# Spreading softmax reciprocals as a high and a low part by two one-pass products instead of one four-byte product

## The reference

```python
def _gqa(q, k, v):
    scale = 1.0 / np.sqrt(q.shape[-1])
    scores = jnp.einsum('bsghd,btgd->bghst', q, k) * scale
    p = jax.nn.softmax(scores, axis=-1)
    return jnp.einsum('bghst,btgd->bsghd', p, v)
...
xout = _gqa(qx, kx, vx).reshape(b, s, nh * d)
cat = jnp.concatenate([core, xout], axis=-1)
catq = _div_clamp_fp8(cat, proj_smooth)
```

## Time and profile before

| what | value |
|---|---|
| median of 3 runs | 2472.32 us (2472.16 to 2473.99) |
| the profiled execution, own time | 2472.09 us |
| its span, first to last instruction | 2470.4 us |
| PE busy | 2306.3 us, 93% |
| DVE busy | 1999.1 us, 81% |
| ACT busy | 1065.0 us, 43% |
| POOL busy | 939.4 us, 38% |
| mean granted clock of TensorE | 0.961 of full speed |

### The profile page before, as it was taken

One profiled execution on the slowest core, in us unless ns is written; L12 is line 12 of the kernel. 1 busy time (PEld: TensorE's weight loads), 2 busy tenths in 40 slices (PEclk: granted clock), 3 DMA queues, 4 the chain that ended last, 5 costly groups with the idle time before them and its releaser, 6 DMA issues. The chain is left out here.

```text
span 2470.4 us, 37732 instructions
## 1 busy us (share of the span) xinstructions
PE 2306.3 (93%) x12485; PEld 2021.7 (82%) x12485; DVE 1999.1 (81%) x3868; ACT 1065.0 (43%) x1824; POOL 939.4 (38%) x640
## 2 busy tenths in 40 slices
PE   7999999999994788867999999999999999999898
PEld 6777777878993566656999999999999999998898
DVE  8999987877774888865888988888889888886347
ACT  1000101015883666641555555555555555554232
POOL 5555200200003244541465556554655555556000
PEclk9999999999996888878999999999999999999999
DMA  9667543335654111124222222212222222114411
GB/s 387 260 274 300 217 150 129 140 147 179 217 171 134 58 60 45 45 60 156 66 90 73 89 78 83 74 50 89 89 74 89 78 85 74 52 62 176 175 53 52
DMA packets 171869, 301.42 MB, mean 122 GB/s; under 512 B 59249, under 2 KB 141250, under 8 KB 166786
## 3 DMA queue, kind: packets, MB, share of 16 engines
q1 hardware_dynamic: 165746, 280.08, 32.9%
q0 software_dynamic: 6032, 20.20, 2.2%
HBM read 211.25 MB, written 89.00 MB: 122 GB/s over the span
## 5 line engine op out<-in xcount | busy, mean ns | idle before, releaser
L1896 PE MATMUL ps<-s_qc,s_ct 128*125 128x448 f32 x2304 | 522.5, 376 | 1.3 <-issue 1.3
L1896 PEld LDWEIGHTS ps<-s_qc,s_ct 128*125 128x125 f32 x2304 | 420.2, 187 | 50.4 <-issue 12.9
L1778 POOL TENSOR_TENSOR keep_x<-keep_x,s_sx 125x896 f32<-125x896 f32 x128 | 287.6, 2247 | 237.5 <-DVE s_mxh L2039 113.7
L572 DVE BATCH_NORM_STATS2 s_st<-ps 125x6 f32<-125x128 f32 x1536 | 318.7, 281 | 55.4 <-PE ps L444 48.9
L1842 ACT ACTIVATE s_sx<-s_sx 125x896 f32<-125x896 f32 x192 | 182.2, 949 | 352.6 <-DVE s_sx L2012 352.6
L1999 DVE TENSOR_TENSOR s_sx<-ps,keep_krs 125x896 f32<-125x896 f32 x192 | 208.9, 1088 | 121.9 <-PE ps L1896 118.4
L1924 PE MATMUL ps<-s_p_hi,s_cn_hi 125*128 125x448 f32 x768 | 284.6, 371 | 2.7 <-DVE s_p_lo L2018 2.7
L1924 PE MATMUL ps<-s_p_hi,s_cn_lo 125*128 125x448 f32 x768 | 281.4, 366 | 0.0
L1924 PE MATMUL ps<-s_p_lo,s_cn_hi 125*128 125x448 f32 x768 | 281.4, 366 | 0.0
L2018 DVE TENSOR_TENSOR s_p_lo<-s_sx,s_p_hi 125x896 fp32r<-125x896 f32 x192 | 256.6, 1336 | 6.9 <-ACT s_p_hi L1847 6.9
L2039 DVE TENSOR_TENSOR s_mxh<-s_mxh,s_sx 125x896 f32<-125x896 f32 x128 | 217.3, 1698 | 0.1
(11 more groups left out here) (378 smaller groups left out, 5033.2 us busy)
## 6 DMA issues: line engine op xcount, KB each, us to landing
l_ahead<-in_ctxt SPq DMA_DIRECT2D x16, 1500.0 KB, 7.8
s_ct<-ct_hi SPq DMA_DIRECT2D x48, 500.0 KB, 4.4
s_ct<-ct_lo SPq DMA_DIRECT2D x48, 500.0 KB, 5.1
s_cn_raw<-in_ctx SPq DMA_DIRECT2D x48, 500.0 KB
l_raw<-in_ctxt SPq DMA_DIRECT2D x15, 1500.0 KB
l_raw<-in_w SPq DMA_DIRECT2D x16, 1024.0 KB, 5.1
ct_hi<-l_hi SPq DMA_DIRECT2D x8, 1500.0 KB, 12.5
ct_lo<-l_lo SPq DMA_DIRECT2D x8, 1500.0 KB, 15.9
```

Source lines behind the costliest of these rows:

```text
L572: ins = dve.bn_stats(st[:, G * t + g, :], kx[0:TT, t % NB, g // 4, DH * (g % 4):DH * (g % 4) + DH])
L1778: pool.tensor_tensor(a, a, p[:, PR * w.pt:PR * w.pt + PR, :], ALU.add).then_inc(s["acc_ready"], 1)
L1896: mm = pe.matmul(sc[st % 2][:, j, :], a[:, k, at:at + TT], x[w.h][:, k, :], start=(c == 0), stop=(c == 5))
```

## The change

DVE rounds `r4` to `fp32r` (`r4_hi`) and subtracts that from `r4` (`r4_lo`), each behind a wait for the instruction ahead of it. ACT builds the diagonal matrices of both parts, so 8 instructions in place of 4. PE spreads them by two `fp32r` products that accumulate, with a copy of the ones in `fp32r`, in place of the one four-byte product.

```diff
-        r4, rdiag, rsc = m.sb("r4", [PAIR, HG]), m.sb("rdiag", [PAIR, HG, PAIR]), m.sb("rsc", [P, QH])
+        r4, r4_hi, r4_lo, rsc = m.sb("r4", [PAIR, HG]), m.sb("r4_hi", [PAIR, HG], F32R), m.sb("r4_lo", [PAIR, HG]), m.sb("rsc", [P, QH])
+        rdiag = m.sb("rdiag", [PAIR, 2, HG, PAIR], F32R)
+        ones_p = m.sb("ones_p", [PAIR, P], F32R)
...
-                        for j in range(HG):
-                            ins = act.activation(rdiag[:, j, :], keep.ident[0:PAIR, 0:PAIR], ACT.Copy, scale=r4[:, j:j + 1])
+                        for part, of in enumerate((r4_hi[:, :].bitcast(F32), r4_lo)):
+                            for j in range(HG):
+                                ins = act.activation(rdiag[:, part, j, :], keep.ident[0:PAIR, 0:PAIR], ACT.Copy, scale=of[:, j:j + 1])
                         ins.then_inc(s["rdiag_ready"], 1)
...
                         pe.wait_ge(s["rdiag_ready"], w.u - 1)
-                        pe.matmul(misc[:, 0:QH], keep.ones[0:PAIR, :], rdiag[:, :, :], start=True, stop=True).then_inc(s["rb_ready"], 1)
+                        for part in range(2):
+                            mm = pe.matmul(misc[:, 0:QH], ones_p[:, :], rdiag[:, part, :, :], start=(part == 0), stop=(part == 1))
+                        mm.then_inc(s["rb_ready"], 1)
...
-                pe.wait_ge(s["ones_ready"], 1)
+                pe.wait_ge(s["ones_ready"], 2)
...
+                dve.tensor_copy(ones_p[:, :], keep.ones[0:PAIR, :]).then_inc(s["ones_ready"], 1)
...
-                        dve.reciprocal(r4[:, :], sums).then_inc(s["r4_ready"], 1)
+                        dve.reciprocal(r4[:, :], sums).then_inc(s["r4_read"], 1)
+                        dve.wait_ge(s["r4_read"], w.u - 1)
+                        dve.tensor_copy(r4_hi[:, :], r4[:, :]).then_inc(s["r4_hi_ready"], 1)
+                        dve.wait_ge(s["r4_hi_ready"], w.u - 1)
+                        dve.tensor_tensor(r4_lo[:, :], r4[:, :], r4_hi[:, :].bitcast(F32), ALU.subtract).then_inc(s["r4_ready"], 1)
```

More of the change, by code:

```diff
@@ L1631, in cross_attention @@
             "sc_ready", "sc_read", "mxh_ready", "mx_ready", "mt_ready", "mt_read", "diag_ready", "mb_ready", "qc_ready", "qc_hi_ready",
-            "qc_lo_ready", "sub_ready", "exp_ready", "hi_ready", "lo_ready", "pv_ready", "acc_ready", "sum_ready", "r4_ready", "rdiag_ready", "rb_ready", "rb_read", "ut_read",
+            "qc_lo_ready", "sub_ready", "exp_ready", "hi_ready", "lo_ready", "pv_ready", "acc_ready", "sum_ready", "r4_read", "r4_hi_ready", "r4_ready", "rdiag_ready", "rb_ready", "rb_read", "ut_read",
             "v_ready", "v_read", "cc_ready", "cat_ready", "cat_stored", "cb_ready", "ce_ready", "cs_ready")}
```

## The result

The changed kernel takes 2603.3 us in the median of 4 runs (2600.92 to 2605.91), the kernel before 2472.24 us on the same chip: a ratio of 1.0529, 95% interval 1.0516 to 1.0542. The prediction, 2606 us and slower, holds. The profiled execution took 2600.92 us with a span of 2599.2 us, 128.8 us more than before.

What follows compares the result with a forecast made beforehand. PE was taken as the bound in the cross attention, pacing DVE. Waits of 105 + 16 us less 12.2 saved gave +109; with 25 for the clock, 2472 + 109 + 25 = 2606 us, range 2530 to 2645.

Steps and rivals of the forecast that it cites:

- The two holds: VectorE's copy waits for POOL's first addition, its subtraction for POOL's next instruction; 72%, 2606 us.
- Sizes: PE's wait before the rdiag product: 5.0 us in odd units, 3.1 in even ones.
- PE's saving: Two fp32r products take 0.42 us instead of 0.80: 0.38 us a unit, 12.2 us in 32 units.
- The clock: Half-speed stretches of 3.4 us behind three in four odd and one in four even pauses: 25 us, bounds 0 and 51.
- The ends: First two and last four units: POOL and reciprocal do not all meet, two pairs counted for three, 16 us.
- PE never pauses there: In the cross attention PE is busy for 200.00 of 200 us, so saved PE time counts in full.
- faster: 2460 us: Rival: PE's saving stands and no wait takes its place; 3% among the cases, 4% for faster overall.
- -4 us: ACT's four more instructions alone, DVE at nothing: odd units wait 0.5 us, 13 x 0.5 + 1 - 12.
- held not at all: Rival: VectorE's four-element instructions pass POOL; PE waits 0.9 and 0.3 us, +6, 2478 us; 8%.
- held once: Rival: only one hold of VectorE's new instructions by POOL; PE waits 2.9 and 2.2 us, +64, 2537 us; 13%.

Runs made afterwards that it cites:

- psum_r4: Changed kernel with the reciprocals r4 written to and read from PSUM instead of SBUF, instruction order unchanged: 2478.36 us, 1.0019 against the kernel before.
- ahead_of_mxh: Changed kernel with VectorE's reciprocal, rounding and subtraction put ahead of step 3's running maximum, whose end releases POOL's first addition: 2476.09 us, 1.0014 against the kernel before.
- second_recip: Changed kernel with r4_hi made by a second reciprocal of the sums in PSUM instead of rounding r4: 2546.36 us, 1.0295 against the kernel before.
- round_first: Changed kernel with POOL's rounding of the older unit put ahead of cn_lo instead of behind it: 2588.71 us, 1.0465 against the kernel before.
- fill_pause: Changed kernel with 12 more one-pass products, result overwritten, in PE's pause before the product with rdiag: 2605.27 us, 1.0543 against the kernel before.
- pe_only: Changed kernel with VectorE's reciprocal only, four ACT instructions, both PE products reading the same matrix (result counts double): 2466.22 us, 0.997 against the kernel before.
- act_and_pe: Changed kernel with VectorE's reciprocal only, ACT's eight instructions making both parts from r4 (result counts double): 2466.62 us, 0.9977 against the kernel before.
- the best version: Changed kernel, VectorE's split ahead of mxh, ACT's rdiag in step 3, PE's transposes behind the fourth context product: 2471.05 us, 0.9986 against the kernel before.
- before_ca: Kernel before, with VectorE's multiplication ca moved up in step 0, behind the score scaling instead of behind p_lo: 2493.54 us, 1.0084 against the kernel before.

## Why the prediction was right

**The two holds** came as written, one after the other, with the right releasers: by the first addition, then by `cn_lo` in odd and by POOL's rounding in even units, in all of units 2 to 27. psum_r4 and ahead_of_mxh take both away, second_recip one, round_first shortens one, and the time follows each. The Trainium skill's rule that the prediction quoted (SBUF — State Buffer, section "SBUF: two separate sides") says that a VectorE instruction with two SBUF inputs is held by a GpSimd one that reads SBUF and started first; the trace agrees down to four elements (2.26 us in place of 0.16), which no row of before showed. That the rounding of `r4`, with one input in SBUF, is held too was read from the earlier trace rows and is so (2.12 us).

**Sizes.** From the end of the reciprocal to PE's product the odd unit takes 1798.38 - 1791.50 = 6.88 us where it took 1730.31 - 1728.33 = 1.98: 4.90 later, predicted 5.0. ACT's end alone is 5.54 later, predicted 5.55; PE then starts 0.05 us behind it, where 0.1 was estimated. The even unit takes 1757.12 - 1751.55 = 5.57 where it took 2.63: 2.94, predicted 3.1. Here ACT's end is 4.25 later, predicted 4.35: POOL's two records overlap by 0.04 us, which the prediction did not count, and the rest is a few hundredths.

**PE's saving and the pair.** A unit from even to odd without half clock lasts 1718.03 - 1678.29 = 39.74 us, 4.65 more than before; predicted 5.0 - 0.38 = 4.62. From odd to even no unit of the changed kernel is without half clock; the 37.81 us of fill_pause, with the same chain, are 2.5 more than the 35.29 of before, predicted 2.72. So a pair grows by 7.2 us in place of 7.34. PE's two products, expected 0.21 us apart, start 0.20 us apart in pe_only and 0.31 behind a pause at full clock.

**The clock.** This term was mis-sized. All 13 odd pauses in units 2 to 27 and 5 of the 13 even ones are followed by half clock; predicted were three in four and one in four. A stretch of 3.4 us costs 1.5 us, not 1.7: 39.26 - 37.81 above, and in the changed kernel itself 1798.38 - 1757.12 = 41.26 us with half clock against 39.74 without. Of a pair's 79.78 us, 79.78 - 39.74 - 37.81 = 2.2 are the clock's, 29 us in 13 pairs, predicted 25 in all. That these are near is luck in part: there were 18 stretches where 15 were counted, and each of 3.4 us was cheaper. The reading from the earlier trace rows that a pause of 2.4 us leaves the clock alone does not hold as a rule: fill_pause's pauses of 2.40 us are mostly followed by half clock.

**The ends.** From unit 2 to unit 28 the time grew by 121.8 us (1279.13 to 2315.73 in place of 1272.95 to 2187.79), outside by 7.0. The prediction had 95 + 25 inside and 109 - 95 = 14 outside. The misses, 2 us too few inside and 7 too many outside, have opposite signs and leave 2606 against 2603.

**One step was wrong without weight.** "PE never pauses there, so a PE time that is saved is worth its full length": its weight loads waited 0.3 to 0.4 us for `ca` in every second unit, and pe_only saves 7.4 us (0.3%) where 12.2 were counted. Under the new pauses this wait is hidden, so the sum did not feel it; the rival "faster: 2460 us" was out of reach while `ca` stood where it does. The "-4 us" for ACT's four instructions without the holds came out as -5.7 (act_and_pe, 0.9977), but by luck: PE's saving was 7.4 and not 12.2 us, and a pair lasts 70.0 us in both act_and_pe and pe_only, so ACT's four instructions cost almost nothing in place of 7.5: their wait replaces the one for `ca`. The "held not at all" sum of 2478 came out as 2478.36 (psum_r4), "held once" at 2537 as 2546, short by the clock, which was left out of it.

## What to carry to other kernels

Before adding a small VectorE instruction, look at what GpSimd starts at the same moment, and at what it has queued behind that: with its data in SBUF the small instruction lasted here until GpSimd's ended, once for each link of a dependent chain. Put such links ahead of the instruction that releases GpSimd, or keep their input in PSUM; here the one took back 128 of 131 us and the other 126, without touching the arithmetic. That only removes the loss: the best version is 0.14% ahead of the kernel before. And read the waits of the weight loads too before calling TensorE the bound: a row of 200.00 in 200 hid them here.

## What the runs showed of the hardware that was not expected

Which engine is held is settled by hundredths of a microsecond: `p_lo` that begins 0.07 us ahead of `cn_lo` costs VectorE nothing, and begun 0.46 us behind it lasts 2.87 us in place of 1.08; the rounding of `r4` loses by 0.05 us. So an instruction moved ahead of others can turn the order further on, and in before_ca 0.6 us of work in another place cost 21 us.

Half clock (1.2 GHz) came behind pauses of 2.40 us in fill_pause and of 2.79 us in the changed kernel, each time in some units and not in others of the same length (1875.65 above is followed by full clock, 1796.60 by half). What tells them apart was not settled.
